# Two hidden layers of an FFN as three fp32r products each, with the order of all engines written anew

## What is computed

```python
x = x + layernorm(attn(moe(x)))          # routed experts, then a banded attention
x = x + ffn(ln(attention(ln(x)) @ Wout)) # 16 heads of 64, position bias, null key

def attention(xn):                       # per batch
    q, k, v = xn @ Wq, xn @ Wk, xn @ Wv  # q: 16 heads x 64, k, v: 64, shared
    sim = l2norm(q) * q_scale @ (l2norm(k) * k_scale).T * 8 + bias
    return softmax(masked(sim)) @ v      # 128 x 129 per head, one null key

def ffn(x):                              # 128 -> 512 -> 512 -> 512 -> 128
    h = silu(x @ w1.T * s1) * (x @ w2.T * s2)
    h = gelu(h @ h1.T * t1)              # layer l2 of the kernel
    h = gelu(h @ h2.T * t2)              # layer l3
    return h @ w3.T * s3
```

## Time and profile before

| | us |
|---|---|
| median of 3 runs | 925.25 |
| lowest and highest | 922.39, 925.89 |
| the profiled execution | 924.58 |
| its span, first to last instruction | 922.9 |

### The profile page before, as it was taken

The page is one execution under the profiler, slowest core; times in us unless marked ns, Lnnn a source line. Parts: engine busy times, 40 slices in busy tenths (PEclk is TensorE's granted clock), DMA queues, the critical chain, the costliest instruction groups (busy, mean ns, idle before and its releaser), DMA issues. The chain is left out here.

```text
span 922.9 us, 15824 instructions
## 1 busy us (share of the span) xinstructions
PE 856.7 (93%) x4992; PEld 556.7 (60%) x4992; DVE 570.4 (62%) x1562; ACT 600.5 (65%) x1600; POOL 445.3 (48%) x388
## 2 busy tenths in 40 slices
PE   4967979899999999899999999899999999799987
PEld 3734556555766557565766557565766557554766
DVE  5588787945777466945667456955578367643410
ACT  2234856678748886578747876478756876597822
POOL 2027857634466436644375345655285344934200
PEclk9869989999999999999999999999999999799999
DMA  6060000000100001000100001000010000000000
GB/s 226 1 220 12 2 14 2 1 1 1 38 1 1 1 1 39 1 1 1 29 10 1 1 1 39 1 1 1 1 38 1 1 1 13 1 1 1 12 6 7
DMA packets 15584, 16.92 MB, mean 18 GB/s; under 512 B 1408, under 2 KB 13072, under 8 KB 15120
## 3 DMA queue, kind: packets, MB, share of 16 engines
q1 hardware_dynamic: 15504, 15.92, 5.4%
HBM read 13.81 MB, written 2.11 MB: 17 GB/s over the span
## 5 line engine op out<-in xcount | busy, mean ns | idle before, releaser
L594 POOL TENSOR_TENSOR sb_sm<-sb_sm,sb_rden 128x512 f32<-128x512 f32 x128 | 136.1, 1066 | 296.0 <-DVE sb_rden L1055 295.7
L1042 DVE SCALAR_TENSOR_TENSOR sb_sm<-ps_S,sb_rq,sb_biasm 128x129 f32<-128x129 f32 x512 | 143.5, 343 | 118.3 <-PE ps_S L1259 110.1
L685 ACT ACTIVATE sb_sm<-sb_sm,sb_nmx 128x129 f32<-128x129 f32 x512 | 198.7, 392 | 12.3 <-DVE sb_nmx L1050 11.8
L587 POOL TENSOR_TENSOR sb_biasm<-sb_bias,sb_maskn 128x512 f32<-128x512 f32 x128 | 164.2, 1298 | 22.4 <-DVE sb_sm L1042 13.8
L1309 PE MATMUL ps_M<-sb_hA,sb_h 128*128 128x512 f32 (+1 forms) x288 | 115.3, 546 | 0.0
L1309 PE MATMUL ps_M<-sb_hB,sb_h 128*128 128x512 f32 (+1 forms) x288 | 115.2, 550 | 0.0
L692 ACT ACTIVATE sb_pT<-ps_T 128x512 f32<-128x512 f32 x128 | 75.3, 591 | 53.8 <-PE ps_T L1267 53.8
L1259 PE MATMUL ps_S<-sb_k,sb_qs 64*128 64x129 f32 x1024 | 94.2, 303 | 17.2 <-DVE sb_sm L1042 15.7
L1259 PEld LDWEIGHTS ps_S<-sb_k,sb_qs 64*128 64x128 f32 x1024 | 70.0, 191 | 59.8 <-issue 57.2
L577 POOL TENSOR_TENSOR sb_rq<-sb_qss,sb_mhalf 128x16 f32<-128x16 f32 x32 | 93.4, 2943 | 17.6 <-DVE sb_qss L1028 17.6
L685 ACT ACTIVATION_READ_ACCUMULATOR sb_sm<-sb_sm,sb_nmx 128x1 f32 x512 | 97.1, 190 | 0.0
(11 more groups left out here) (211 smaller groups left out, 1468.2 us busy)
## 6 DMA issues: line engine op xcount, KB each, us to landing
sb_xg<-in_xT SPq DMA_DIRECT2D x8, 256.0 KB, 3.6
sb_xs<-in_x SPq DMA_DIRECT2D x8, 256.0 KB, 4.1
sb_qs<-in_xT SPq DMA_DIRECT2D x1, 2048.0 KB, 10.6
sb_h<-in_h SPq DMA_DIRECT2D x2, 1024.0 KB, 9.4
out_y<-sb_res SPq DMA_DIRECT2D x7, 256.0 KB, 2.6
sb_sm<-toeplitz SPq DMA_DIRECT2D x1, 1024.0 KB, 5.9
sb_rows<-in_rows SPq DMA_DIRECT2D x1, 648.0 KB, 6.5
sb_oT<-in_wq SPq DMA_DIRECT2D x1, 512.0 KB, 10.2
```

The lines of the kernel that those rows point to most:

```text
L587: pool.tensor_tensor(biasm[:, heads, 1:NK], bias0[:, heads], maskn[:, j // 4].unsqueeze(1).broadcast_to([128, 4, S]), ALU.add)\
L594: pool.tensor_tensor(sm[:, heads, 1:NK], sm[:, heads, 1:NK], rden[:, heads].unsqueeze(2).broadcast_to([128, 4, S]), ALU.mult)\
L685: ins = act.activation(sm[:, h], sm[:, h], ACT.Exp, bias=nmx[:, h:h + 1], accum_out=den[:, h:h + 1])
L1042: ins = dve.scalar_tensor_tensor(sm[:, h], bank(g, "sim", j, odd)[:, m * NK:(m + 1) * NK], rq[:, k * HEADS + h:k * HEADS + h + 1], biasm[: ...
```

## The change

**Layers.** `h1` and `h2` exist as high and low fp32r parts, and l2 and l3 multiply with `three`. `gated` writes back to `al`; the new ACT steps h1.0-3 (`high1`) copy `al` to the high part `hAs[0]`, the new DVE steps (`low1`) write `hAs[1]`. In the same way `gelu2` writes `al`, then h2.0-3 (`high2`, `low2`) write `hBs`. `gelu3` and l4 stay in fp32 with `hA`.

**Space.** `n3` is now `hA[:, 0]`, `zT` the first tile of `hBs`, `xnT` is `yT`, the raw h1 and h2 are loaded one after the other to `hA`, and the scratch of the prologue moves from `hB` to `pT`. With it come waits of ln3's norm for l4 and of zT's copies for l3 of the group before. The scratch for software DMA is set to 1024.

**Loads and splitting of h1 and h2.** SP's new step hw.0 (end of the fill) loads h1 when routing is done, hw.1 (end of the start pass's list) loads h2 when h1 has been split; ph.4-5 and pl.4-5 split them in the start pass.

**Squares of q** go to four places (two of `hT`, two of `gs`); the wait is for the sum of the tile four back, and the third square of a group waits for mix.

**x1** stays where it was written, in place g mod 3; the two moves are gone.

**Fill.** The step warm.k issues two matmuls of `ident` by `ident` into a bank of ring T that nobody reads; there are 22 such steps. The bias goes through two banks instead of four.

**Order.** All lists are new. The core of the diff:

```diff
 "pe fill"
-        lg.0 rw.0 exp.0-2 pb.0 exp.3 pb.1 exp.4 down.0 pb.2 lg.1-2 qkv.0 lg.3 scores.0 lg.4-7 pb.3 mix.0 fl.0
-        xnT.0 fl.1-2 q.0 fl.3 q.1 kv.0 qs.0 q.2 qs.1 q.3-4 qs.2-3 q.5-6 qs.4-5 q.7 qs.6-7 kT.0 qst.0
+        lg.0 pb.0 warm.0-2 pb.1 warm.3-4 lg.1 rw.0 exp.0 lg.2-3 exp.1 lg.4 exp.2 lg.5 pb.2 exp.3 lg.6-7 exp.4
+        down.0 pb.3 warm.5 qkv.0 scores.0 warm.6-7 mix.0 warm.8-10 fl.0-1 warm.11-12 fl.2 warm.13 xnT.0
+        warm.14-15 fl.3 q.0-1 kv.0 warm.16 qs.0-1 q.2-4 qs.2-3 q.5-6 qs.4-5 q.7 qs.6 warm.17 qs.7 warm.18 qst.0
+        kT.0 warm.19-21
 "pe steady"
-        rw.0 sim.0 exp.0 sim.1 exp.1-2 sim.2 exp.3 sim.3 exp.4 down.0 PT.0 sim.4 zT.0 PT.1 sim.5 qkv.0 l1.0 PT.2
-        sim.6 l1.1-3 PT.3 l2.0 PV.0 sim.7 scores.0 l2.1 PT.4 sim.8 z.0 PT.5 l2.2 sim.9 PV.1 PT.6 l2.3 mix.0
-        sim.10 l3.0 PT.7 sim.11 PV.2 z.1 PV.3 sim.12 PT.8 l3.1-2 z.2 PT.9 sim.13 l3.3 xnT.0 PT.10 z.3 sim.14
-        PV.4 q.0-1 sim.15 PT.11 kv.0 qs.0 l4.0 qs.1 q.2-3 PT.12 q.4 PV.5 qs.2 z.4 qs.3-4 q.5-7 qs.5 kT.0 qs.6
-        PT.13 qs.7 PT.14 z.5 qst.0 PT.15 PV.6-7 z.6-7
+        rw.0 sim.0 exp.0 sim.1 exp.1 sim.2 exp.2-3 sim.3 exp.4 down.0 zT.0 PT.0 sim.4 PT.1 qkv.0 l1.0 sim.5 l1.1
+        PT.2 l1.2 PT.3 l1.3 sim.6 PV.0-1 sim.7 scores.0 l2.0-2 PT.4 mix.0 z.0 PT.5 sim.8 l2.3 PT.6 sim.9 z.1
+        PV.2 sim.10 l3.0 PT.7 l3.1 sim.11 l3.2 xnT.0 PT.8 z.2 sim.12 PT.9 l3.3 sim.13 PV.3-4 sim.14 PT.10 q.0
+        kv.0 sim.15 q.1 z.3 PT.11 q.2 l4.0 PT.12 q.3 z.4 PV.5 qs.0-3 q.4-5 PT.13 q.6-7 PT.14 qs.4-7 z.5 qst.0
+        PT.15 PV.6-7 kT.0 z.6-7
 "act steady"
-        xh.0 rw.0 exp.0-4 ex.0-2 PT.0 down.0 zT.0 ex.3 PT.1 qkv.0 l1.0 PT.2 l1.1-3 ex.4-5 PT.3 PV.0 l2.0 PT.4
-        ex.6 l2.1 PT.5 ex.7 PT.6 l2.2 PV.1 l2.3 ex.8 PT.7 ex.9 PV.2 ex.10 l3.0 PV.3 PT.8 l3.1 ex.11 PT.9 l3.2-3
-        xnT.0 PT.10 ex.12 q.0 PV.4 q.1 ex.13-14 PT.11 q.2-3 ex.15 PT.12 q.4-7 PV.5 PT.13-15 kT.0 PV.6-7
+        xh.0 exp.0 rw.0 exp.1-4 ex.0-2 down.0 zT.0 ex.3 qkv.0 l1.0 PT.0 h1.0 l1.1 PT.1 l1.2 h1.1 PT.2-3 l1.3
+        ex.4 h1.2-3 PV.0 ex.5-6 PV.1 l2.0 h2.0 l2.1 h2.1 PT.4 l2.2 PT.5 h2.2 ex.7 l2.3 h2.3 PV.2 PT.6 ex.8 PT.7
+        ex.9 l3.0-1 ex.10-11 xnT.0 PT.8 l3.2 PT.9 PV.3 l3.3 ex.12 q.0 PV.4 q.1 ex.13 PT.10 q.2 PT.11 ex.14 q.3
+        ex.15 PT.12 q.4 PV.5 PT.13 q.5-7 PT.14-15 PV.6-7 kT.0
...
 "dve steady"
+        rw.0 xl.0 ln3.0 sim.0 exp.0 sim.1 max.0 exp.1-2 sim.2 exp.3 max.1 exp.4 inv.0 max.2 zT.0 sim.3 inv.1
+        down.0 max.3 zl.0 inv.2-3 sim.4 max.4 qkv.0 l1.0 h1.0 l1.1 sim.5 h1.1 l1.2-3 sim.6 max.5-6 h1.2-3
+        scores.0 inv.4-5 sim.7 inv.6 h2.0 mix.0 h2.1 sim.8 max.7 h2.2 sim.9 max.8 inv.7 max.9 h2.3 sim.10 ln1.0
...
 "act drain"
-        zT.0 l1.0-3 l2.0-3 l3.0-3
+        zT.0 l1.0-1 h1.0-1 l1.2-3 h1.2-3 l2.0-1 h2.0-1 l2.2 h2.2 l2.3 h2.3 l3.0-3
 "sp fill"
-        maskn.0 rw.0
+        rw.0 maskn.0 hw.0
 "sp start"
-        rw.0 maskn.0
+        rw.0 maskn.0 hw.1
...
-        h1, h2, w3 = sb("h1", [128, NO, HID]), sb("h2", [128, NO, HID]), sb("w3", [128, NO, D])
+        h1, h2 = ([sb(name + n, [128, NO, HID], f32r) for n in "hl"] for name in ("h1", "h2"))
...
-        sq = hT[:, 0:2]
+        sq = [hT[:, 0], hT[:, 1], gs[:, 0], gs[:, 1]]
...
+            def load_square(g, k):
+                sp.wait_ge(*((routed, 2 * ROUTE_OPS), (parts_low["h1"], 1))[k])
+                fetch(("h1", "h2")[k], raw["h1"])
...
-                act.wait_ge(ssq_psum.sem, ssq_psum.at(g, max(c - 1, 0)))
-                act.activation(sq[:, c % 2], bank(g, "q", c)[:], ACT.Square).then_inc(q_squared.sem, 1)
+                act.wait_ge(ssq_psum.sem, ssq_psum.at(g, max(c - 3, 0)))
+                if c == 2:
+                    act.wait_ge(mix_psum.sem, mix_psum.at(g, 1))
+                act.activation(sq[c % 4], bank(g, "q", c)[:], ACT.Square).then_inc(q_squared.sem, 1)
...
+                act.wait_ge(l2_ready.sem, l2_ready.at(g, 0))
...
+            def high1(g, o):
+                act.wait_ge(l1_gated.sem, l1_gated.at(g, o + 1))
+                act.wait_ge(l4_psum.sem, l4_psum.at(g, 0))
+                t = tokens(g)
+                act.activation(hAs[0][:, o, t], al[:, o % 2, t], ACT.Copy).then_inc(l1_high.sem, 1)
...
+            def high2(g, o):
+                act.wait_ge(l2_gelu.sem, l2_gelu.at(g, o + 1))
                 act.wait_ge(l3_psum.sem, l3_psum.at(g, 0))
                 t = tokens(g)
-                act.activation(hB[:, o, t], bank(g, "l2", o)[:, t], ACT.Gelu, scale=h1s[:, o:o + 1]).then_inc(l2_ready.sem, 1)
+                act.activation(hBs[0][:, o, t], al[:, o % 2, t], ACT.Copy).then_inc(l2_high.sem, 1)
...
+            def low1(g, o):
+                dve.wait_ge(l1_gated.sem, l1_gated.at(g, o + 1))
+                dve.wait_ge(l1_high.sem, l1_high.at(g, o + 1))
+                t = tokens(g)
+                low(hAs[1][:, o, t], al[:, o % 2, t], hAs[0][:, o, t], None, l1_ready)
...
+            def warm(g, k):
+                pe.wait_ge(const, 3)
+                for n in range(2):
+                    pe.matmul(banks["T", 0][:, 0:128], ident[:], ident[:], start=True, stop=True)
...
-                        ins = pe.matmul(ps[:, t], w[:, c, o * 128:(o + 1) * 128], src[:, c, t], start=(c == 0), stop=(c == NO - 1))
+                        ins = three(ps[:, t], [part[:, c, o * 128:(o + 1) * 128] for part in w], [part[:, c, t] for part in src],
+                                    c == 0, c == NO - 1)
```

## The result

| | us |
|---|---|
| median of 4 runs, changed | 865.47 (862.27 to 869.56) |
| median of 4 runs, before, on the same chip | 924.04 (922.39 to 925.89) |
| ratio, 95% interval | 0.9368, 0.932 to 0.9416 |
| the profiled execution, changed | 863.99, its span 861.9 |

The change makes the kernel faster, as forecast, by 58.6 us instead of 36. The busy times by pass (PE, PEld, DVE, ACT, POOL, then clock, DMA share, GB/s) answer to the earlier trace rows: the fill in two pieces, the start pass, a steady pass, the stretch from the last qst to l4d (l4 of the first half of group 7), and the end.

A forecast was written before the change was run, and what follows sets the result against it. PE was taken to set the period, busy for 102.79 of 105.13 us in a steady pass. The terms summed as 924.6 - 33.2 - 2.0 - 1.1 + 1.8 - 3 + 1.5 = 888.6, stated as 888, range 876 to 905.

The forecast's parts named there:

- l2 and l3 on PE: Layers l2 and l3, seven full-width groups: three fp32r products replace each fp32 one, 4.75 us gained per group, -33.2.
- The parts on ACT and DVE: Copy and subtraction per h tile: ACT 76.8, DVE at most 73.7 us of 100; charged 0.3 us per steady pass.
- rival A: In every pass PE waits 2 to 4 us on low parts or the reordered softmax; 910 us, chance 0.10.
- Rival B: Slower: a DVE low part queued behind a waiting reduction or score exposes 10.4 us a pass; 971 us, chance 0.04.
- The order: New step order in steady passes: covers the new copies and low parts with 1 to 2 us to spare; no gain counted.
- the chain: Latency of copy and subtraction ahead of l2 and l3: 0.3 us per steady pass, six times, +1.8 (-2 to +6).
- The start pass: First full pass: splitting h1 and h2 on ACT and DVE amid the scores costs +1.5 us (0 to +5).
- The last pass and the end: Group 7, split in two halves: -2.0 us for the first, in the last pass, and -1.1 net in the drain.
- rival D: New order also removes 2.2 us of waits per steady pass and 8.9 us idle in the last; 870 us, chance 0.07.
- Fill: Before the passes: bias ahead of experts, lg.1 ahead of rw, filler matmuls; q stage earlier, -3 us (-8 to +3).
- The term of 2 us for the clock: In the fill, filler matmuls and lg work in gaps keep experts from starting at half clock, returning about 2 us.
- Squares in four places: Late in the pass ACT may run three tiles ahead of qs instead of one; worth nothing, since PE does not wait.

The follow-up runs named there:

- experiment 5: Changed kernel without copies and subtractions for the h tiles, l2 and l3 taking the high part in all three products: 858.69 us, 98.2 a steady pass.
- Experiments 2: Changed kernel's code with the old order lists, new steps put behind those they follow, no filler: 931.47 us, 105.2 a steady pass.
- experiment 3: Changed kernel's code in the old order, l2 and l3 using and awaiting only high parts, low parts computed but left out: 928.6 us, 105.0 a pass.
- experiment 6: Changed kernel with each ACT copy of an h tile made twice: 873.94 us, 99.3 a steady pass.
- experiment 4: Changed kernel's code in the old order, high parts only in l2 and l3, without copies and subtractions: 889.27 us, 100.07 a steady pass.
- experiment 7: Changed kernel with the eight qs of PE's steady passes set apart between other kinds of step: 898.46 us, 103.3 to 105.2 a pass.
- experiment 10: Changed kernel with the old order in the start pass alone, new steps put in: 871.82 us, start pass 79.87.

## Why the prediction was right or wrong

**l2 and l3 on PE: right.** The term was -4.75 a group; the line measured -4.64, and the whole pass in the old order -5.1, where PT (0.3), qkv and scores (0.2) also got cheaper. Loads of weights are covered: l2 has 0.2344 from start to start with new weights for each matmul. The statement of the Trainium skill that loads run ahead of matmuls in flight (TensorE: Matmul & The Clock Gate, Architectural detail) agrees with that.

**The parts on ACT and DVE: right for this order, for a reason that isn't shown to carry.** I charged 0.3 us a steady pass; experiment 5 gives 0.5, so rival A's 2 to 4 us did not come. Of the difference between the two traces, 0.38 are the unexplained time at PT.7 and 0.3 are listed waits (2.46 against 2.16). ACT's estimate of 76.8 and DVE's of 73.7 at most stand beside 75.5 and 71.4, and the new order has ten table loads. But I reckoned ACT's slack as a mean, 77 of 100 us. Experiments 2 to 4 show that the same parts with about the same mean cost 4.9 us a pass under the old lists. Rival B, a result slower than before, came about there, with the whole pass back at 105.2. Its mechanism was not the one I named, a low part queued behind a reduction: with no wait on low parts at all (experiment 3) the loss stayed. That ACT is full in mid-pass goes with the loss in experiments 2 and 3, but experiment 6 has it fuller and loses 0.6. So which steps of the old lists make the parts cost 4.9 us stays open, and so does the share of DVE's subtractions, as experiment 4 takes both away.

**The order: the step that failed.** The prediction took the order as something that only costs: +0.3 for the chain in a steady pass, +1.5 in the start pass, and PE's other work at its old price. I had used the price of a hand-over, 0.10 us for the first matmul behind another kind, for the six stretches of the layers, and not for the rest of the list. With equal layers and no parts the new order is worth 1.9 us a steady pass (100.07 against 98.2), eleven of the 25 us missed. With the parts in (100.07 against 98.79 in the pass read), 1.3 us of it are left, and the work by kind has them as qs in 2 stretches instead of 7 (0.7), PT (0.5, although PT.7 lost 0.38), PV in pairs (0.3), z, l4, q, kv and mix (0.7), against 0.7 more in l1, the rw select, sim and experts and 0.25 of waiting. Only the grouping of qs was tested by itself (experiment 7); for the other kinds the cheaper neighbours are read from the traces, not shown by a run.

**The start pass: wrong in sign.** +1.5 was forecast, -7.2 came. I saw 11.4 us of idle PE there and counted it as cover for the splits, not as something that an order can take away. At an equal clock the order is worth 5.7 us (experiment 10). The profiled execution also had a clock of 1.00 there, against 0.96 before, which goes with another 1.4 us against the 0.98 of experiments 5 and 7. That part is luck of one execution: the same lists took up to 75.5. PE's idle time fell from 11.4 us to 8.2, its waits on scores from 5.0 to 3.4; the waits after:

```profile
PE ps_S L1289 <- DVE sb_sm L1057: 3.4, 5, 1.2
PE ps_M L1246 <- DVE sb_hT L971: 2.7, 1, 2.7
PE ps_T L1297 <- POOL sb_sm L605: 1.0, 1, 1.0
```

**The last pass and the end.** -9.5 came for -6.8, and -1.9 for -1.1. The layers' line fell by 6.4 us in the first of these stretches, near the 4.75 + 2.0 of the sum. PE's waits there fell from 8.9 to 6.6 us. That is a quarter of the 8.9 us that rival D takes away there. Its other half did not come: the steady waits did not go, 2.5 us against 2.2. D's 870 came nearest, by a gain of another kind.

**Fill: right in sum, partly by luck**, -2.9 for -3. rw started at 20.68 instead of 14.29, 6.4 us lost where 4 to 5 were named. The wait for the bias fell to 2.73 us from 5.80 and did not go. q started at 58.37, before the 60 named, and the fill ended at 74.36, before the 79 named. The term of 2 us for the clock rests on a misreading: in the kernel before, the experts (15.7 to 28.8 us) ran at the full clock of 2.4 GHz. The half clock of 1.2 GHz stood later, where PE was busy for 8.0 of 16 us and waited for the bias:

```profile
14.29:38.00 23.71, 22.02 (x90) 15.04 (x90) 15.60 (x32) 9.05 (x16) 3.23 (x6) 1.00 0.19 77
42.00:58.00 16.00, 7.97 (x28) 5.67 (x28) 10.82 (x41) 2.63 (x4) 3.85 (x5) 0.50 0.57 202
```

The mean clock from the first rw on did rise, from 0.84 to 0.97. The row of the wait for the bias (timeline of PE):

```profile
50.69 3.38 PE L1164 MATMUL ps_S<-sb_sm,sb_pT 128*128 128x512 f32 x4 [2.73 <-DMA sb_sm<-toeplitz]
```

**Squares in four places: the use was missed.** I found them worth nothing, since no wait on squares was there to remove. By the code they allow a stretch of four qs to stand late, and experiment 7 prices what that avoids: 2.1 us of work that got dearer and a 2.2 us wait for a bank. No run has the new order with two places, so their own share stays open.

In sum, 12.8 of the 25 us are in the steady passes, 8.7 in the start pass (1.4 of it the clock), 2.7 in the last and 0.8 at the end. My range was too narrow on the side of the gain because D's condition was read off the waits alone.

## What to carry to other kernels

Where an engine is busy for 97% of a pass, a new order still has a value that no view of waits shows: take the distance from start to start of each kind by its neighbours, and count the stretches of both lists. Don't price extra work on a second engine by its busy time, neither as a mean nor in its fullest slices: the copies and subtractions cost 0.5 us a pass under one set of lists and 4.9 under the other, and ACT at 29.55 of 30 us cost 0.6 in experiment 6. Compare single passes only beside their granted clock. And test an order crossed with the edit that came with it, since here neither the edit under the old order (105.2) nor the order under the old layers (102.3) gives their joint gain (98.66).

## What was not expected of the hardware

- Four 128x128 transposes on PE (a PT) cost 0.59 us between two qs, mostly 0.53 ahead of sim, qs or PV, 0.44 between z and an fp32 layer product, and 0.36 between two fp32r stretches, at recorded durations of 0.60 to 0.66 each time.
- One qs, four fp32 products of 128x128 onto 32 rows, costs 0.36 us alone and 0.25 in a stretch of four.
- A change of function on ACT took 1.283 us in the traces of the kernel before, the changed one and experiments 2 to 4, and the next function started right behind it (load at 376.05, exponential at 377.34 in the changed kernel).
- The start pass with the same lists took 72.8 us at a mean granted clock of 1.00, 74.2 at 0.98 and 75.5 at 0.95.
